# Moving the residual sum of a feed-forward's output from GpSimd to TensorE, with ScalarE copying the sum out

## What is computed

```python
def fp4_linear(x, w):
    xq = fp4_quant_dequant(x)
    wq = fp4_quant_dequant(w)
    return jnp.einsum('bsk,nk->bsn', xq, wq)
gate = fp4_linear(x, w_gate)
y = fp4_linear(x, w_up)
h = jax.nn.silu(gate) * y
return fp4_linear(h, w_down)
...
g = _silu(_L1_ffn_ref(xn, L1_ffn_w_gate, L1_ffn_w_up, L1_ffn_w_down))
x = x + s * g
```

## Time and profile before

| | |
|---|---|
| median of 3 runs | 1036.28 us (1034.65 to 1038.63) |
| the profiled execution's own time | 1034.11 us |
| its span, first to last instruction | 1032.3 us |
| mean granted PE clock | 0.881 of 2.4 GHz |
| the last phase in the span | from 888 us to the end, some 144 us |
| busy over the whole span | PE 804.6, DVE 806.2, ACT 612.8, POOL 397.3 us |

### The profile page before, as it was taken

How to read it: one execution, slowest core, us unless ns; L and a number is a source line. 1 busy time by engine, 2 the same in 40 slices (tenths; PEclk the granted TensorE clock), 3 DMA queues, 4 the chain that set the end, 5 groups by cost and what they waited for, 6 DMA issues and landing times. The chain is left out here.

```text
span 1032.3 us, 23120 instructions
## 1 busy us (share of the span) xinstructions
PE 804.6 (78%) x6866; PEld 472.2 (46%) x6866; DVE 806.2 (78%) x1738; ACT 612.8 (59%) x1270; POOL 397.3 (38%) x684
## 2 busy tenths in 40 slices
PE   4888899999806788888896455649999999776764
PEld 3643333333305677776775233313333333345553
DVE  6758899999666345565663899889999998799984
ACT  3866677777705366566653478747777777433342
POOL 6852343333413666676673132231111211022332
PEclk9977999999955899999998666659999999888987
DMA  4692422222102343343342145532222221000001
GB/s 138 230 305 65 140 78 84 73 74 78 32 6 59 115 145 119 122 124 123 122 129 95 61 142 169 175 126 66 69 76 64 75 66 33 1 1 21 13 19 30
DMA packets 114716, 94.52 MB, mean 92 GB/s; under 512 B 10783, under 2 KB 102714, under 8 KB 114512
## 3 DMA queue, kind: packets, MB, share of 16 engines
q1 hardware_dynamic: 109104, 83.31, 25.9%
q0 software_dynamic: 4608, 8.93, 2.9%
q10 hardware_dynamic: 928, 1.32, 0.4%
HBM read 59.18 MB, written 34.08 MB: 90 GB/s over the span
## 5 line engine op out<-in xcount | busy, mean ns | idle before, releaser
L1157 ACT ACTIVATE pr<-score 128x512 f32<-128x512 f32 x512 | 279.1, 599 | 109.7 <-PE score L1225 109.6
L387 DVE TENSOR_REDUCE neg_max<-bank 128x2 f32<-128x512 f32 x480 | 303.7, 683 | 7.5 <-PE bank L371 6.3
L1225 PE MATMUL score<-qs,ks 51*128 51x256 bf16 x1024 | 179.3, 277 | 13.5 <-DVEq L1132 5.6
L371 PE MATMUL bank<-ks,qs 48*128 48x256 bf16 x960 | 168.4, 278 | 0.0
L1243 PE MATMUL p_o<-pr,vs 128*18 128x256 f32 x2048 | 164.2, 391 | 0.6 <-ACT pr L1157 0.6
L1225 PEld LDWEIGHTS score<-qs,ks 51*128 51x128 bf16 x1024 | 64.8, 95 | 155.7 <-DVE neg_max L387 49.3
L396 POOL TENSOR_TENSOR max_parts<-neg_max,one 128x16 bf16<-128x16 f32 x64 | 14.3, 223 | 268.6 <-DVE neg_max L387 259.9
L1428 POOL DMA_INDIRECT y_scratch<-y_all,to_i x72 | 79.9, 1109 | 56.0 <-DVE y_all L1529 45.1
L1644 ACT ACTIVATE hid<-p_ha,b_slot 128x128 f32<-128x128 f32 x144 | 44.9, 364 | 89.8 <-PE p_hd L1755 63.3
L1422 POOL DMA_INDIRECT y_all<-hn_scratch,token_i x72 | 76.1, 1056 | 55.6 <-DVEq L1510 34.0
L1529 DVE COPY y_all<-p_y 128x128 f32<-128x128 f32 x72 | 20.9, 290 | 83.3 <-PE p_y L1766 40.5
(11 more groups left out here) (324 smaller groups left out, 1645.0 us busy)
## 6 DMA issues: line engine op xcount, KB each, us to landing
w_now<-w_dram SPq DMA_DIRECT2D x72, 256.0 KB
ks<-k_scratch SPq DMA_DIRECT2D x128, 96.0 KB, 2.2
qs<-q_scratch SPq DMA_DIRECT2D x128, 96.0 KB, 2.3
k_scratch<-parts SPq DMA_DIRECT2D x16, 384.0 KB, 2.7
q_scratch<-parts SPq DMA_DIRECT2D x16, 384.0 KB, 3.0
k_scratch<-parts SPq DMA_DIRECT2D x16, 256.0 KB, 2.3
q_scratch<-parts SPq DMA_DIRECT2D x16, 256.0 KB, 2.6
both<-y_scratch SPq DMA_DIRECT2D x8, 512.0 KB, 4.0
```

The source lines that it names most:

```text
L371: return pe.matmul(bk[:, qt * L:(qt + 1) * L], S.qs[u][rows, place(h), qt * P:(qt + 1) * P], S.ks[u][rows, place(h), :], start=True, stop= ...
L387: return dve.tensor_reduce(S.neg_max[:, h // (H // 2), :, col:col + 1], bk[:].rearrange("p (q t) -> p q t", t=L), AX.X, ALU.max, negate=True)
L1157: act.activation(pr[s % N_PR][:, 2 * k:2 * k + 2, :], score[k][:], ACT.Exp, scale=SCALE).then_inc(exp_done, 1)
L1225: scored = pe.matmul(score[k][:, j, :], ks[u][rows, place(h), kt * P:(kt + 1) * P], qs[u][rows, place(h), :], start=True, stop=True)
```

## The change

GpSimd now only multiplies z by s, in place in z, without a wait on the store. PE gets `add_input`: it multiplies the residual's tile by the identity into the p_z bank (512 columns, fp32), waits for the scaled z, and accumulates the identity times z onto it. This runs in `down` between the transposes of the next group's hidden values and that group's down product, which must in turn wait until the bank has been read out. ACT gets `keep_output`, a copy of p_z to o, which waits for the sum and for the store of the previous o. On ACT `hidden` is moved ahead of `cut_input`, and `keep_output` stands between them. SP still waits for `out_ready`, which ACT now gives; the last group is made by DVE as before.

```diff
--- before.py
+++ after.py
@@ -2181,6 +2181,7 @@
         p_z = S.ps(ctx, "p_z", [P, 512])
         steps_x, steps_h = sem("steps_x"), sem("steps_h")
         x_split, x_cut, h_split, h_cut, o_scaled = (sem(n) for n in ("x_split", "x_cut", "h_split", "h_cut", "o_scaled"))
+        summed = sem("summed")
         names = ("z_scaled", "h_rounded", "xq_ready", "xq_turned", "xt_ready", "gate_full", "up_full",
                  "gate_ready", "up_free", "hq_ready", "hq_turned", "ht_ready", "z_done", "z_ready", "out_ready", "stored")
         (z_scaled, h_rounded, xq_ready, xq_turned, xt_ready, gate_full, up_full, gate_ready, up_free,
@@ -2210,18 +2211,15 @@
 
         @block.gpsimd
         def _(pool):
-            def output(g):
+            def scale_output(g):
 
                 z3 = z[g % 2][:].rearrange("p (n c) -> p n c", c=D)
                 pool.wait_ge(z_ready, g + 1)
-                pool.wait_ge(stored, g * 16 + 16)
-                pool.tensor_tensor(o[:], z3, S.s_all[:, now(g), :], ALU.mult).then_inc(z_scaled, 1)
-                pool.wait_ge(z_scaled, g + 1)
-                pool.tensor_tensor(o[:], o[:], S.x_all[:, now(g), :], ALU.add).then_inc(out_ready, 1)
+                pool.tensor_tensor(z3, z3, S.s_all[:, now(g), :], ALU.mult).then_inc(z_scaled, 1)
 
             def turn(g, first, last):
                 if g >= 2:
-                    output(g - 2)
+                    scale_output(g - 2)
                 if last:
                     return
                 pool.wait_ge(h_rounded, g + 1)
@@ -2230,7 +2228,7 @@
                 fp4_value(pool, hn[:], NH, amax_h[g % 2], hq[:]).then_inc(hq_ready, 1)
 
             turns(turn)
-            output(NG - 2)
+            scale_output(NG - 2)
 
         @block.vector
         def _(dve):
@@ -2345,8 +2343,13 @@
             def output(g):
                 act.wait_ge(z_done, g + 1)
                 if g >= 2:
-                    act.wait_ge(z_scaled, g - 1)
+                    act.wait_ge(summed, g - 1)
                 act.activation(z[g % 2][:], p_z[:], ACT.Silu).then_inc(z_ready, 1)
+
+            def keep_output(g):
+                act.wait_ge(summed, g + 1)
+                act.wait_ge(stored, g * 16 + 16)
+                act.copy(o[:].rearrange("p n c -> p (n c)"), p_z[:]).then_inc(out_ready, 1)
 
             def cut_input(g):
                 act.wait_ge(x_split, g)
@@ -2361,10 +2364,12 @@
                 if not last:
                     inputs(g + 1)
                     silu(g + 1, 0)
+                if not first:
+                    hidden(g - 1)
+                if g >= 2:
+                    keep_output(g - 2)
                 if g + 2 < NG:
                     cut_input(g + 2)
-                if not first:
-                    hidden(g - 1)
                 cut_hidden(g)
                 if not first:
                     output(g - 1)
@@ -2375,6 +2380,7 @@
             silu(0, 0)
             turns(turn)
             hidden(NG - 1)
+            keep_output(NG - 2)
             output(NG - 1)
 
         @block.tensor
@@ -2398,6 +2404,13 @@
                                          start=True, stop=True)
                     last.then_inc(full, 1)
 
+            def add_input(g):
+
+                flat = lambda t: t.rearrange("p n c -> p (n c)")
+                pe.matmul(p_z[:], S.ident, flat(S.x_all[:, now(g), :]), start=True, stop=False)
+                pe.wait_ge(z_scaled, g + 1)
+                pe.matmul(p_z[:], S.ident, z[g % 2][:], start=False, stop=True).then_inc(summed, 1)
+
             def down(g):
                 pe.wait_ge(hq_ready, g + 1)
                 for n in range(NT):
@@ -2405,9 +2418,12 @@
                         turned = pe.transpose(p_t[i][0:w, n * P:(n + 1) * P], hq[:, n * I2 + lo:n * I2 + lo + w],
                                               S.ident)
                 turned.then_inc(hq_turned, 1)
+                if g:
+                    pe.wait_ge(z_ready, g)
+                    add_input(g - 1)
                 pe.wait_ge(ht_ready, (g + 1) * 3)
                 if g:
-                    pe.wait_ge(z_ready, g)
+                    pe.wait_ge(out_ready, g)
                 for n in range(NT):
                     for i, (_, w) in enumerate(K_CHUNKS):
                         last = pe.matmul(p_z[:, n * D:(n + 1) * D], hq_t[0:w, i, n * P:(n + 1) * P],
```

## The result

The changed kernel takes 1032.01 us (median of 22 runs, 1027.81 to 1040.83); the kernel before, beside it, 1036.82 (22 runs, 1033.52 to 1040.4). The ratio is 0.9961, with a 95% interval of 0.9946 to 0.9976: 0.4% faster, some 4 us. That is small, but the interval leaves out 1. The forecast was 1035.6, range 1032.0 to 1040.5, so the median lies inside by 0.01 us.

The account below looks back on a forecast made before the run. VectorE was taken to set the pace of the last phase. Terms +1.57 - 2.97 - 0.76 + 1.0 - 0.95 + 1.45 = -0.66 us on the profiled 1034.11; against the median, 1035.6, range 1032.0 to 1040.5.

Parts of the forecast that it names:

- -2.97: Turns 2 to 5: VectorE's stall behind GpSimd's sum goes, about 0.75 us a turn, 2.97 us saved in all.
- Rivals 2 and 3: 2: turns 2 to 5, VectorE waits for p_up, +2.3, chance 0.12; 3: input's cut late there, +8.2, chance 0.09.
- Rival 4: Turns 2 to 5: VectorE's stall at GpSimd's scaling goes too, turn 1's cost hidden; sum -5.4 us, chance 0.07.
- Turn 1, +1.57: Turn 1: the input's cut stands behind the hidden copies and VectorE has no slack, 1.57 us lost once.
- Turn 6, -0.38: Turn 6: GpSimd's sum no longer delays a small VectorE instruction, 0.38 us saved; nothing booked for the 1.10 p_up wait.
- rival 1: Turn 6: VectorE slips in ahead of GpSimd's queued scaling, a further -0.69 us, sum -1.35, chance 0.22.
- Turn 7, +1.0: Turn 7: cut_hidden stands behind keep_output, after half-clock transposes and slowed adds; 1.0 us lost (0.3 to 2.0).
- The lock's -0.95: Behind turn 7: with one GpSimd operation left, one of two long VectorE operations loses its delay, 0.95 us saved.
- The tail, +1.45: After the last hq: adds and copy stand ahead of the last product, 1.45 us lost (0.75 full clock, 2.5 half).
- the first-come rule: Shared port of VectorE and GpSimd: first to issue holds it, so waiting VectorE precedes queued GpSimd work; -0.69 us, chance 0.22.

Follow-up runs that it names:

- a2: The kernel before with GpSimd's sum left out, nothing added on PE or ScalarE: 1032.16 us against 1037.71, ratio 0.9971.
- a3: The changed kernel with GpSimd's scaling of z by s left out too: 1026.98 us against 1037.71 for the kernel before, ratio 0.9915.
- a1: The kernel before with one edit, ScalarE's hidden ahead of cut_input: 1036.45 us against 1037.71, ratio 0.9996.
- a4: The changed kernel with cut_input put back in front of hidden, keep_output behind them: 1031.91 us against 1037.71 for the kernel before, ratio 0.9955.
- c0: The changed kernel once more, no edit: 1031.76 us, ratio 0.9955 to the kernel before.
- c1: The changed kernel with z scaled in front of hq for groups 0 to 4, and group 6's scaling behind the last hq: 1029.45 us, ratio 0.9933.
- c3: The changed kernel with groups 0 to 4 scaled before hq, group 6 wholly on GpSimd after the last hq, two unread PE products in the tail: 1027.99 us.
- b4: The edits of b1, b2 and b3 together on the changed kernel: ratio 0.9941 to the kernel before.
- b3: The changed kernel with group 6 scaled and added wholly on GpSimd, behind VectorE's last hq: ratio 0.9937 to the kernel before.
- b1: The changed kernel with cut_input ahead of hidden in turn 1 alone: ratio 0.9948 to the kernel before.
- b2: The changed kernel with GpSimd's scaling of z for groups 0 to 4 moved in front of hq: ratio 0.9917 to the kernel before.

## Why the prediction was right, and where its steps were not

**The bound and the gain.** Right. VectorE sets the pace, and its second stall was the sum's: -2.97 forecast, -3.02 and -3.00 measured; a2 shows it alone, a3 shows the other stall, a1 and a4 show that PE's order and clock inside these turns are worth nothing. Rivals 2 and 3 did not occur: the cut in turn 2 ended at 930.55, T0+7.2, 1.8 us before VectorE was due. Rival 4 took a3's edit to happen.

**Turn 1, +1.57.** The size was right (1.62 wait, +1.73 in c0), its certainty wrong. The step "There is no slack on VectorE" rests on the place of the transposes (917.08 to 918.65) in one execution in which PE ran at half clock in turn 1; in after's profile PE was at full clock there, ended them 4.84 us behind T0 of turn 0 (c0: 7.67), and the cut was over at 915.74, before VectorE asked for it at 916.90. It is a term with a probability: of the nine profiles with hidden ahead of the cut in turn 1, in four VectorE waited 1.5 to 1.6 us for ScalarE (a1, c0, c1, c3, all at half clock there) and in five it did not wait (all at full clock).

**Turn 6, -0.38.** The failed step is "I book nothing for that, since arriving earlier it only waits longer for z times s". It measured -1.34. The row at 987.57 shows amax_h issued before hq's end (985.16 + 2.59 = 987.75) and finished at 987.82, while the scaling, queued behind hq, did not keep it out. This was rival 1. The Trainium skill, SBUF — State Buffer, "Who interferes with whom", has the first to issue take the shared port; the trace agrees, and a2 shows the other side of it. The rival's own size, -0.69 more, was too small: it put the end of L2289 (L2291 before) at T0+4.24, but the scaling was not held up, ended at 988.98, T0+3.90, and L2289 ended at 989.05, T0+3.97, so 0.96 more came. The gain also needs the sum gone: in a1 VectorE slipped in as well, and the sum took the time back from hn.

**Turn 7, +1.0.** Did not occur in after or c0, where turn 7 and the last hq moved by -1.32 = -0.37 - 0.95. The lock's -0.95 was right: L263 still 2.57, the last hq 1.62. The wrong step is half clock for the transposes of hq(6) (2.80 taken, 1.53 measured): they came behind 2.07 us of idle time, not 2.44, and PE kept its clock. PE was at full clock in turn 6 in before too, and whether the shorter idle time is the reason is not shown. Where the transposes were slower (c1 1.72, c3 1.65, b4 2.08), the term appeared: turn 7 took 12.96 or 12.97 against b3's 12.33.

**The tail, +1.45.** Measured +0.93 and +1.64: adds at nearly full clock in after, slower in c0, inside the stated bounds of 0.75 and 2.5. What the step left out is that the tail of before is itself one draw: its 9.55 is the shortest of the six without adds or throw-away products (the others 10.67 to 11.89), because its last product ran at full clock over the gap. The seven tails with adds took 10.46 to 11.46. Against a usual tail of before the adds may cost nothing.

**In sum**, -0.66 against -4.22 and -2.04 in two profiles, and about -4 by the ratio. The forecast came out too slow because terms that rest on half clock (turn 1, the cut of turn 7) often came out at full clock, and because the first-come rule was given 0.22 when it held wherever the case arose: in after, a1, a2 (turn 7), a4, b1, b3 and c0 VectorE came 0.17 to 0.19 us before hq's end, with the scaling queued, and took 0.23 to 0.25. Both errors point the same way. That the median still lies in the range is luck, by 0.01 us at the lower end; c0's, 1031.76, lies below it. What was right is the mechanism of turns 2 to 5 and its size, and that the whole effect is small.

## What to carry to other kernels

An operation of GpSimd beside VectorE is not free even when nothing waits for its result: look for tiny VectorE instructions of several times their usual length and for a GpSimd instruction ending with them. Moving it away is one cure, worth 3.0 us in turns 2 to 5 here; moving what is left beside a VectorE instruction with an operand in PSUM is another, which took 2.7 us more from these turns (b2) for a stretch of 0.14 us a turn. Before counting a faster PE stretch as a gain, check that the bound engine waits for it; and in the head and tail of a pipeline, where it does, price each PE step at both clocks, in the kernel before as well as in the one after.

## What the runs showed of the hardware

The same kernel was granted different clocks in the same place in different executions: p_gate in turn 1 took 1.45 in after and 2.71 in c0, and turn 1 was 1.7 us longer in c0. In the six profiles with half clock there the piece before T0 of turn 0 took 22.6 to 23.1 us, in the eight with full clock 23.3 to 24.1, so counts from T0(0) on can overstate by up to about 1 us what such an execution loses. In turns 1 to 5, down products behind a gap of 1.75 us or less took 2.92 to 2.95 in every kernel, and those behind 2.3 to 4.5 us took 4.2 to 5.5. In turn 7 and the tail an empty gap of 1.64 to 1.73 went with either. With work that nobody reads in the gap the last product took 2.92 instead of 4.55, as it did in all seven kernels with the adds there. What decides in a single execution whether a gap of 1.7 us costs the clock is not settled by these runs.
